# Two output stores of a routed low-rank layer move to the activation engine's DMA queue, one of them as half the rows of the last store

## What is computed

```python
base = jnp.einsum('btd,od->bto', x, W)
logits = jnp.einsum('btd,ed->bte', x, Wr)          # + 5.0 at the sequence's own id
topw, topi = jax.lax.top_k(logits, 2)
weights = jax.nn.softmax(topw, axis=-1)
gates = jnp.sum(jax.nn.one_hot(topi, E) * weights[..., None], axis=-2)
h = jnp.einsum('btd,erd->bter', x, A)
lora_out = jnp.einsum('bter,bte,eor->bto', h, gates, B)
return x + base + 2.0 * lora_out
```

## Time and profile before

| | |
|---|---|
| time, median of 3 runs | 81.17 us (80.80 to 81.37) |
| profiled execution, its time | 80.93 us |
| profiled execution, its span | 79.1 us |
| TensorE matmul busy | 74.6 us, 94% of the span |
| VectorE busy | 51.1 us, 65% |
| ScalarE busy | 22.6 us, 29% |
| GpSimd busy | 22.8 us, 29% |
| HBM written | 4.19 MB |

### The profile page before, as it was taken

One profiled execution on the slowest core, in us unless ns is written; L12 is line 12 of the kernel. 1 busy time (PEld: TensorE's weight loads), 2 busy tenths in 40 slices (PEclk: granted clock), 3 DMA queues, 4 the chain that ended last, 5 costly groups with the idle time before them and its releaser, 6 DMA issues.

```text
span 79.1 us, 1625 instructions
## 1 busy us (share of the span) xinstructions
PE 74.6 (94%) x505; PEld 70.5 (89%) x505; DVE 51.1 (65%) x216; ACT 22.6 (29%) x57; POOL 22.8 (29%) x25
## 2 busy tenths in 40 slices
PE   6996999799999999999999999999999999999960
PEld 2376998799998999999999999999999999999950
DVE  0183898878588828466482928284664979787670
ACT  4329931514221414050231314140503113111200
POOL 4034880063360141506050513315060605000000
PEclk9999999999999999999999999999999999999999
DMA  1999991597399479999810000270000008032124
GB/s 14 305 375 382 428 425 71 90 419 294 50 373 377 56 301 434 402 244 408 345 71 0 0 0 0 99 298 0 0 0 0 0 37 360 0 133 93 39 102 167
DMA packets 3748, 14.23 MB, mean 180 GB/s; under 512 B 416, under 2 KB 1056, under 8 KB 3488
## 3 DMA queue, kind: packets, MB, share of 16 engines
q1 hardware_dynamic: 3600, 13.98, 47.4%
q10 hardware_dynamic: 144, 0.20, 0.8%
HBM read 9.99 MB, written 4.19 MB: 179 GB/s over the span
## 4 chain that ended last, share of the span: by engine, by line
PE 78%; DMA 7%; DVE 6%; SPq 2%; ACT 1%; issue 1%; DVEq 0%
PE heads_ps L402 36%; PE base_ps L402 25%; DMA first_sb<-in_first 7%; PE heads_ps L434 5%; PE base_ps L434 5%; PE ghT_ps L425 2%; PE base_ps L438 2%; PE heads_ps L438 2%; DVE b_lo L359 2%; DVE w_lo L342 1%; SPq L167 1%; ACT w_hi L224 1%; SPq L165 1%; DVE out_sb L328 1%; ACT x_hi L221 1%
## 5 line engine op out<-in xcount | busy, mean ns | idle before, releaser
L205 POOL TENSOR_TENSOR x_lo<-xT_sb,x_hi 128x512 fp32r<-128x512 f32 x14 | 18.5, 1318 | 39.0 <-ACT x_hi L231 39.0
L402 PE MATMUL heads_ps<-w_hi,x_hi 128*128 128x392 f32 x64 | 22.7, 361 | 0.6 <-ACT w_hi L224 0.6
L402 PE MATMUL heads_ps<-w_hi,x_lo 128*128 128x392 f32 x64 | 21.6, 340 | 0.0
L402 PE MATMUL heads_ps<-w_lo,x_hi 128*128 128x392 f32 x64 | 21.5, 340 | 0.0
L402 PE MATMUL base_ps<-w_hi,x_lo 128*128 128x256 f32 x64 | 18.0, 281 | 0.0
L402 PE MATMUL base_ps<-w_hi,x_hi 128*128 128x256 f32 x64 | 17.8, 283 | 0.0
L402 PE MATMUL base_ps<-w_lo,x_hi 128*128 128x256 f32 x64 | 17.8, 280 | 0.0
L402 PEld LDWEIGHTS heads_ps<-w_hi,x_hi 128*128 128x128 f32 x64 | 12.0, 190 | 1.9 <-ACT x_hi L221 1.3
L235 ACT ACTIVATE ghT_hi<-ghT_ps 128x128 fp32r<-128x128 f32 x15 | 4.1, 277 | 30.9 <-PE ghT_ps L425 30.9
L278 DVE TENSOR_TENSOR ghT_lo<-ghT_ps,ghT_hi 128x128 fp32r<-128x128 f32 x15 | 4.4, 290 | 12.7 <-ACT ghT_hi L235 12.6
L402 PEld LDWEIGHTS base_ps<-w_lo,x_hi 128*128 128x128 f32 x64 | 12.1, 189 | 0.0
(11 more groups left out here) (43 smaller groups left out, 92.0 us busy)
## 6 DMA issues: line engine op xcount, KB each, us to landing
x_sb<-in_x SPq DMA_DIRECT2D x4, 768.0 KB, 5.6
out<-out_sb SPq DMA_DIRECT2D x4, 768.0 KB, 3.9
xT_sb<-in_xT SPq DMA_DIRECT2D x3, 768.0 KB, 4.3
first_sb<-in_first SPq DMA_DIRECT2D x3, 454.0 KB, 5.1
xT_sb<-in_xT SPq DMA_DIRECT2D x1, 1024.0 KB, 6.4
x_sb<-in_x SPq DMA_DIRECT2D x1, 1024.0 KB, 9.5
out<-out_sb SPq DMA_DIRECT2D x3, 256.0 KB, 2.0
xT_sb<-in_xT SPq DMA_DIRECT2D x1, 256.0 KB, 6.0
```

The lines of the kernel that those rows point to most:

```text
L205: nc.gpsimd.tensor_tensor(x_lo[:, s, :], xT_sb[:, t - len(FIRST), :], x_hi[:, s, :].bitcast(FP32), ALU.subtract).then_inc(x_lo_made, 1)
L402: return nc.tensor.matmul(dst, xs[:, s, chunks[k]], ws[:, k, cols], start=(k == 0 and n == 0), stop=(k == KC - 1 and n == 2))
```

## The change

Tile 14's store is issued by ScalarE, behind its last activation, with a wait for `out_made` of 15. The last store, columns 0 to 255 of tile 15, is cut into rows: SyncE issues rows 0 to 63, ScalarE rows 64 to 127, each behind a wait for `out_made` of 16. The store of columns 256 to 511 of tile 15 stays with SyncE. SyncE's last instruction waits for ten stores now. No instruction of TensorE, VectorE or GpSimd differs.

```diff
-            for t in range(GROUPED, TILES - 1):
+            for t in range(GROUPED, TILES - 2):
                 sp.wait_ge(out_made, t + 1)
                 store(t, 1)
 
             sp.wait_ge(heads_read, TILES)
             sp.dma_start(out[:, TILES - 1, BASE:O], out_sb[:, TILES - 1, BASE:O]).then_inc(out_stored, 16)
             sp.wait_ge(out_made, TILES)
-            sp.dma_start(out[:, TILES - 1, 0:BASE], out_sb[:, TILES - 1, 0:BASE]).then_inc(out_stored, 16)
-            sp.wait_ge(out_stored, 16 * (GROUPS + TILES - 1 - GROUPED + 2))
+            sp.dma_start(out[0:P // 2, TILES - 1, 0:BASE], out_sb[0:P // 2, TILES - 1, 0:BASE]).then_inc(out_stored, 16)
+            sp.wait_ge(out_stored, 16 * (GROUPS + TILES - 1 - GROUPED + 3))
...
             ghT_upper(TILES - 2, (TILES - 2) % SLOTS)
             ghT_upper(TILES - 1, (TILES - 1) % SLOTS, warm_ps)
+            act.wait_ge(out_made, TILES - 1)
+            act.dma_start(out[:, TILES - 2, :], out_sb[:, TILES - 2, :]).then_inc(out_stored, 16)
+            act.wait_ge(out_made, TILES)
+            act.dma_start(out[P // 2:P, TILES - 1, 0:BASE], out_sb[P // 2:P, TILES - 1, 0:BASE]).then_inc(out_stored, 16)
```

## The result

| | before | changed |
|---|---|---|
| time, median of 20 runs | 81.34 us (80.80 to 81.97) | 81.78 us (81.27 to 82.79) |
| ratio | | 1.006, 95% interval 1.0039 to 1.0081 |
| profiled execution, its time | 80.93 us | 81.78 us |
| its span | 79.1 us | 80.0 us |

The changed kernel is slower by 0.6%: 0.44 us by the medians, 0.49 us by the ratio. That is within the 1% of "same", but clear of noise, and the median lies 0.08 us above the range of the prediction. One of the changed kernel's runs (82.79 us) was a slow one and isn't in the ratio, and among the profiles of the experiments one, that of ScalarE's even rows alone, is of a slow execution (82.70 us).

A forecast was written before the change was run, and what follows sets the result against it. TensorE, busy for 94% of the span, was taken as the bound, so only the 2.1 us tail could move. Terms 0 + 0 + 0.04 + 0 = +0.04 us, set on the median 81.17, gave 81.2 us, range 80.7 to 81.7.

The forecast's parts named there:

- SyncE was not the holdup: Tail: SyncE idles between issues; the rival that it was the holdup saved 0.34 us, giving 80.8, chance 0.02.
- tile 14's store costs nothing on ScalarE: Tail: moving this issue off SyncE saves 0 and costs 0, with the same issue start, 75.81.
- both halves are issued in one moment: Last store: a sign that both half stores are issued at the same moment, with 0.4 us each.
- the late tile 14: Rival: ScalarE fetches instructions after its last activation, tile 14's store starts 0.9 us late, 81.8 to 82.1; chance 0.09.
- the gain: Rival: over 1% faster by something the profile doesn't show, the tail falling from 2.1 to 1.3 us; chance 0.04.
- "Same", at 0.87: Whole kernel: chance 0.87 that the time stays within about 1%, 0.8 us; faster 0.04, slower 0.09.
- Three of the prediction's own signs of being wrong: Tail: wrong if under 1.9 or over 2.4 us, or halves land over 0.2 apart; issues expected at 0.4 each.
- The last store is cut by rows: Last store: two half stores side by side add only issue time, 0.41 instead of 0.37, so +0.04 us.
- half pace would cost nothing: Last store's data: 64 rows moving at half the pace costs nothing while both halves run together.
- The rival of halves that come apart at half pace: Last store: issues served in turn, second half 0.37 us late, 81.3, or 81.5 at half pace; chance 0.14.
- The "above" bound of 0.37: Last store: upper bound on the cut's cost, +0.37 us, if the two issues are served one after the other.

The follow-up runs named there:

- ScalarE's even rows alone: Kernel before, but ScalarE stores only the 64 even rows of the last store and the odd rows are not stored: ratio 1.003 (1.0003 to 1.0056).
- 96 and 32 rows: Changed kernel with the last store cut at row 96 instead of 64, SyncE storing 96 rows and ScalarE 32: ratio 1.0046 (1.0019 to 1.0073).

## Why the prediction was wrong

What held: SyncE was not the holdup and issues the upper columns 0.03 us behind their producer (76.42 + 0.42 = 76.84, issue at 76.87); tile 14's store costs nothing on ScalarE (0.9998); both halves are issued in one moment; the late tile 14 and the gain didn't come. "Same", at 0.87, came true because a loss of 0.6% is under 1%, and not because nothing was lost. Three of the prediction's own signs of being wrong appeared: the tail is 2.7 us and not at most 2.4, the halves land 0.3 us apart and not at most 0.2, and their issues take 0.55 and 0.58 us and not 0.4.

What failed is the second part of the sum, "The last store is cut by rows", +0.04. It took the issue as 0.41, and start-up, data and completion as unchanged, from rows that all have 128 rows, though it said itself that no row shows a 64-row store. From the issue to the last landing it was 0.8 + 0.5 + 0.4 = 1.7 us before, and is 1.2 + 0.7 + 0.4 = 2.3 us now:

- Start-up to first data, 0 taken beyond the 0.04 of the issue: about +0.4. This is the larger term. The issue lies in it, with 0.55 and 0.58 measured instead of 0.37, +0.2. It is there on either engine, alone or in a pair, in adjacent or every second row (1.1 to 1.2 us), and none of 32, 48, 80, 96 and 128 rows shows it.
- Data, 0 taken: 0.7 instead of 0.5, +0.2. The prediction had both halves run together, so that half pace would cost nothing. But the second queue's half moves behind the first's, and each takes about 0.4 us, as ScalarE's half does where the other isn't stored (78.8 to 79.2). The rival of halves that come apart at half pace comes nearest to this; what it had wrong is the reason, an issue served in turn, for the issues start together and only the data is in turn. This trace agrees with the Trainium skill, page "SBUF — State Buffer", section "Door 1: The DMA port swizzle (why `[64,N]` ≈ `[32,N]`)", by which partitions 0 to 63 reach eight of the sixteen DMA ports and 64 to 127 the other eight: 64 adjacent rows moved at 215 GB/s, every second row of 128 at 338.
- Completion, 0 taken: unchanged.

The same sum fits the others: 0.8 + 0.6 + 0.4 = 1.8 us for the cut by columns, 0.8 + 0.7 + 0.5 = 2.0 for 96 and 32 rows. Of the 0.6 us in the profile the runs show 0.44 to 0.49. The "above" bound of 0.37 was too low for that, since it added one further issue and neither start-up nor data.

The miss of 81.78 against 81.2 has a second source: 0.17 us of it is the baseline, 81.17 from three runs and 81.34 from twenty. Set on 81.34, the same range would have ended at 81.87 and held the result, so that the median fell just outside is partly chance; the missing 0.4 us in the sum is not.

What stays open: why 64 rows of all counts are slow to issue and to start, and why the data of two stores that are issued at once on two queues moves one behind the other.

## What to carry to other kernels

In a tail that is one store long, look first whether the issuing engine is idle between its issues: here it was, and a second queue had nothing to save. Cutting a store doesn't cut its start-up and completion, and a new shape brings its own: a shape that no row of the trace shows deserves a wider range, or a profile of its own first. If a store must be cut over two queues, the cut by columns at full height (tail 2.25 us, ratio 1.002) cost least here and the cut into 64 adjacent rows most (2.7 us, 1.0056), though the intervals of the two ratios overlap.

## What had not been expected of the hardware

- A store of 64 rows, of 256 or 512 columns, takes 0.49 to 0.59 us to issue and 1.1 to 1.2 us to its first data; 32, 48, 80, 96 and 128 rows, each alone, take 0.32 to 0.38 and 0.80 to 0.85.
- The issue behind a 64-row store is slow too: 0.58 for 96 rows, 0.59 for 128.
- 64 adjacent rows alone move at 195 to 225 GB/s in the busiest stretches of 0.1 us, 64 alternate rows at 328 to 338.
- Two stores of 64 KB that SyncE and ScalarE issue in the same moment move one behind the other, SyncE's first in all three cases (adjacent rows, alternate rows, columns), and the second lands 0.2 to 0.3 us later.
